# Attention with exact row maxima: 4 of a group's 32 maxima units are read as one difference and one sum

## What is computed

```python
q = split_heads(_tlin(x, w_q, s_q, b_q))        # (8, 16 heads, 1024, 16)
k = split_heads(_tlin(x, w_k, s_k, b_k))
v = split_heads(_tlin(x, w_v, s_v, b_v))
scores = jnp.einsum('bhqd,bhkd->bhqk', q, k) / jnp.sqrt(jnp.float32(HEAD))
attn = jax.nn.softmax(scores, axis=-1)
ctx = jnp.einsum('bhqk,bhkd->bhqd', attn, v)
```

## Time and profile before

| | before |
|---|---|
| median of three executions | 1980.98 us |
| span of the profiled execution | 1981.5 us |
| TensorE busy | 1931.0 us (97%) |
| VectorE busy | 1845.4 us (93%) |
| ScalarE busy | 1652.1 us (83%) |
| GpSimd busy | 750.0 us (38%) |
| granted TensorE clock, mean | 0.997 |

### The profile page before, as it was taken

How to read it: one execution, slowest core, us unless ns; L and a number is a source line. 1 busy time by engine, 2 the same in 40 slices (tenths; PEclk the granted TensorE clock), 3 DMA queues, 4 the chain that set the end, 5 groups by cost and what they waited for, 6 DMA issues and landing times.

```text
span 1981.5 us, 43034 instructions
## 1 busy us (share of the span) xinstructions
PE 1931.0 (97%) x15806; PEld 1131.4 (57%) x15806; DVE 1845.4 (93%) x3236; ACT 1652.1 (83%) x3241; POOL 750.0 (38%) x747
## 2 busy tenths in 40 slices
PE   8999999999999999999999999999999999999998
PEld 7766444444444444444444444444478888888876
DVE  4788999999999999999999999999289999999997
ACT  6655889899898989989898988988967777777776
POOL 3000364666575353010001001000046666666785
PEclk9999999999999999999999999999999999999999
DMA  7985553355435435433543544353011111111210
GB/s 224 284 236 209 120 76 52 62 95 96 94 81 102 95 80 99 93 94 82 101 96 78 97 94 94 82 100 98 28 49 49 49 49 49 49 49 56 63 33 27
DMA packets 127199, 181.46 MB, mean 92 GB/s; under 512 B 37836, under 2 KB 82636, under 8 KB 126988
## 3 DMA queue, kind: packets, MB, share of 16 engines
q1 hardware_dynamic: 119308, 171.10, 37.6%
q10 hardware_dynamic: 7392, 7.34, 1.1%
q0 software_dynamic: 288, 0.27, 0.1%
HBM read 103.68 MB, written 73.40 MB: 89 GB/s over the span
## 4 chain that ended last, share of the span: by engine, by line
DVE 63%; PE 32%; issue 3%; DMA 1%; ACT 1%; SPq 0%; DVEq 0%; POOLq 0%; POOL 0%; ACTq 0%
DVE halfmax L1135 50%; PE ps L1401 10%; DVE halfmax L1130 7%; PE ps L1440 6%; PE ps L494 4%; PE ps L504 3%; PE ps L1389 2%; PE ps L1412 2%; PE ps L1045 1%; PE ps L1011 1%; PE ps L481 1%; PE ps L1448 1%; DVE room L1591 1%; PE ps L1457 1%; DVE room L1678 1%
## 5 line engine op out<-in xcount | busy, mean ns | idle before, releaser
L1096 ACT ACTIVATE room<-ps 128x512 f32<-128x512 f32 x2048 | 1084.4, 600 | 125.0 <-PE ps L1011 103.0
L1135 DVE TENSOR_REDUCE halfmax<-ps 128x1 f32<-128x512 f32 x1714 | 1039.5, 676 | 1.3 <-PE ps L986 1.3
L1011 PE MATMUL ps<-qs,ks 50*128 50x512 f32 x2048 | 716.4, 448 | 2.4 <-DVE halfmax L1135 1.3
L986 PE MATMUL ps<-ks,qs 48*128 48x512 f32 x1960 | 667.6, 437 | 23.8 <-DVE halfmax L1130 22.3
L1045 PE MATMUL ps<-room,vals 128*17 128x256 f32 (+2 forms) x8192 | 578.9, 384 | 0.3 <-ACT craw L1104 0.3
L986 PEld LDWEIGHTS ps<-ks,qs 48*128 48x128 f32 x1960 | 314.5, 185 | 423.6 <-DVE halfmax L1135 309.2
L164 POOL CAST mrow<-turned_rows 128x32 fp32r<-128x32 f32 x32 | 6.7, 210 | 904.2 <-DVE turned_rows L159 695.4
L1011 PEld LDWEIGHTS ps<-qs,ks 50*128 50x128 f32 x2048 | 327.2, 184 | 22.9 <-ACT room L1096 14.5
L1045 PEld LDWEIGHTS ps<-room,vals 128*17 128x17 f32 x8192 | 167.4, 96 | 232.9 <-issue 168.1
L1401 PE MATMUL ps<-wguT,xqT 128*128 128x512 f32 (+1 forms) x1152 | 268.4, 386 | 3.9 <-DVE xqT L1631 3.9
L1401 PEld LDWEIGHTS ps<-wguT,xqT 128*128 128x128 f32 x1152 | 212.0, 189 | 51.8 <-issue 9.9
(11 more groups left out here) (116 smaller groups left out, 2212.1 us busy)
## 6 DMA issues: line engine op xcount, KB each, us to landing
qk_parts<-parts SPq DMA_DIRECT2D x64, 512.0 KB, 3.9
qs<-qk_parts SPq DMA_DIRECT2D x192, 128.0 KB, 4.4
ks<-qk_parts SPq DMA_DIRECT2D x192, 128.0 KB, 7.1
ctx_raw<-craw SPq DMA_DIRECT2D x64, 256.0 KB
ready<-passing SPq DMA_DIRECT2D x27, 512.0 KB, 6.5
pairs<-ready SPq DMA_DIRECT2D x27, 512.0 KB
out_dram<-fin SPq DMA_DIRECT2D x64, 128.0 KB, 1.7
xin<-in_L_attn_x_dram ACTq DMA_DIRECT2D x14, 512.0 KB, 5.4
```

What stands on the lines that cost most here:

```text
L986: nc.tensor.matmul(ps[:, MX + max_number(i, u, bank) % 4, :], qs[rows, i.slot(RING), pair, t * P:(t + 1) * P], ks[rows, i.slot(RING), pair ...
L1011: nc.tensor.matmul(ps[:, score_bank(i, s, n), :], ks[rows, slot, pair, kt * P:(kt + 1) * P], qs[rows, slot, pair, qh * BANK:(qh + 1) * BAN ...
L1096: nc.scalar.activation(prob[:, prob_slot(i, s), score_order(i, s)[n], :], ps[:, score_bank(i, s, n), :], ACT.Exp, scale=float(D) ** -0.5). ...
L1135: nc.vector.tensor_reduce(halfmax[:, i.slot(2), bank, column:column + 1], ps[:, at + bank, :], AX.X, ALU.max, negate=True).then_inc(max_re ...
```

## The change

Units 1, 9, 17 and 25 of groups 2 to 31 are handled in another way ("folded", `FOLD_PER = 8`, `FOLD_AT = 1`): 120 units in all, none of them among the units whose two banks are read in one reduce.

- TensorE makes bank 0 with two products into the same bank: the negated queries (`minus_q`) with the second half of the keys, then the queries with the first half. The bank holds the difference first minus second. Bank 1 is made as before.
- ScalarE takes the positive part of bank 0 (Relu) into `excess` in SBUF, between the third and the fourth exponential of the step. That also releases bank 0 to TensorE.
- VectorE waits for that and for bank 1, and with one instruction over 512 elements adds both, negates the sum and reduces it to its minimum, which is the negated maximum of all 1024 scores. The two reduces of the unit are gone. The other column of `halfmax` is set to a large number once.
- GpSimd negates the queries of the upper half of the rows once for each group (`minus_q`, 48 x 1024 elements), behind the wait for that group's stack and ahead of the wait for the turned maxima of the group before. Its first call of `next_maxima` now stands behind the wait for the projections.

```diff
+    minus_q = sb("minus_q", [P, 2, S], F32R)
+    excess = sb("excess", [P, 2, BANK])
...
+    def folded(i, u):
+        return i.k > 1 and u % FOLD_PER == FOLD_AT
...
+    def bank_read(eng, tile):
+        k, u = units_in_order[tile // QH]
+        if folded(At(None, k, RING), u) and tile % QH == 0:
+            eng.wait_ge(excess_ready, fold_number[k, u] + 1)
+        else:
+            eng.wait_ge(max_read, reads_done[tile])
...
             if max_number(i, u, bank) >= 4:
-                pe.wait_ge(max_read, reads_done[max_number(i, u, bank) - 4])
+                bank_read(pe, max_number(i, u, bank) - 4)
...
+            if folded(i, u) and bank == 0:
+                pe.wait_ge(minus_ready, i.k - 1)
+                nc.tensor.matmul(ps[:, MX + max_number(i, u, bank) % 4, :],
+                                 minus_q[rows, i.slot(2), t * P:(t + 1) * P],
+                                 ks[rows, i.slot(RING), pair, BANK:2 * BANK], start=True, stop=False)
+                nc.tensor.matmul(ps[:, MX + max_number(i, u, bank) % 4, :],
+                                 qs[rows, i.slot(RING), pair, t * P:(t + 1) * P],
+                                 ks[rows, i.slot(RING), pair, 0:BANK],
+                                 start=False, stop=True).then_inc(max_psum, 1)
+                return
...
+        def first_over_second(i, u):
+            n = fold_number[i.k, u]
+            act.wait_ge(max_psum, max_number(i, u, 0) + 1)
+            if n >= 2:
+                k, before = folds[n - 2]
+                act.wait_ge(max_read, reads_done[max_number(At(None, k, RING), before, QH - 1)])
+            nc.scalar.activation(excess[:, n % 2], ps[:, MX + max_number(i, u, 0) % 4, :],
+                                 ACT.Relu).then_inc(excess_ready, 1)
...
+                ahead, unit = maxima(i, s)
+                if i.k >= 0 and ahead.ok(NGR) and folded(ahead, unit + 1):
+                    exps(j, t, range(first, GH - 1))
+                    first_over_second(ahead, unit + 1)
+                    first = GH - 1
...
+        def take_folded(i, u):
+            column, at = max_column(u), MX + max_number(i, u, QH - 1) % 4
+            n = fold_number[i.k, u]
+            dve.wait_ge(excess_ready, n + 1)
+            dve.wait_ge(max_psum, max_number(i, u, QH - 1) + 1)
+            nc.vector.tensor_tensor_reduce(excess[:, n % 2], ps[:, at, :], excess[:, n % 2], -1.0, LARGE, ALU.add,
+                                           ALU.min, halfmax[:, i.slot(2), 0, column:column + 1]).then_inc(max_read, 1)
...
+            if i.k > 1:
+                dve.wait_ge(neutral, 1)
...
+                if i.k == 0 and s == ST - AHEAD + 2:
+                    columns = [max_column(u) for k, u in folds if k == folds[0][0]]
+                    nc.vector.memset(halfmax[:, :, 1, columns[0]:columns[-1] + 1:columns[1] - columns[0]],
+                                     LARGE).then_inc(neutral, 1)
...
+        def negate(i):
+            rows = slice(HALF, HALF + KR)
+            pool.wait_ge(stack_in[i.slot(RING)], i.turn(RING, LOADS, LOADS))
+            pool.wait_ge(maxima_out.parted, 2 * group[0])
+            wait(pool, passing_ready, 2 * max(0, min(group[0] - 1 - NG, READY)))
...
+            nc.gpsimd.tensor_scalar(minus_q[rows, i.slot(2), :], qs[rows, i.slot(RING), 0, :].bitcast(F32), -1.0, None,
+                                    ALU.mult).then_inc(minus_ready, 1)
+            pool.wait_ge(minus_ready, i.k - 1)
...
         def next_maxima():
+            if group[0] + 1 < NGR:
+                negate(At(None, group[0] + 1, RING))
             maxima_out.part(nc, pool, At(None, group[0], RING))
...
+        projections_done(pool)
         next_maxima()
-        projections_done(pool)
```

More of the change, by code:

```diff
@@ L54 @@
 FILL = 3
+FOLD_PER = 8
+FOLD_AT = 1
+LARGE = 3.0e38
 TILES_RUN = NTILES + 9
@@ L773, in attend @@
     wgu = sb("wgu", [WB, 2, 8, H])
+    minus_q = sb("minus_q", [P, 2, S], F32R)
+    excess = sb("excess", [P, 2, BANK])
+    minus_ready = sem("minus_ready")
+    excess_ready = sem("excess_ready")
+    neutral = sem("neutral")
     max_psum = sem("max_psum")
@@ L892, in max_number @@
         return QH * item[i.k, u] + bank
+    def folded(i, u):
+        return i.k > 1 and u % FOLD_PER == FOLD_AT
+    fold_number = {which: n for n, which in enumerate((k, u) for k, u in items() if folded(At(None, k, RING), u))}
+    folds = list(fold_number)
+    units_in_order = list(items())
     def read_table():
@@ L898, in read_table @@
         for k, u in items():
-            if whole(At(None, k, RING), u):
+            if whole(At(None, k, RING), u) or folded(At(None, k, RING), u):
                 table += [reads + 1, reads + 1]
@@ L1172, in vector @@
                         take_max(j, u, range(QH))
+                    elif j.ok(NGR) and folded(j, u):
+                        take_folded(j, u)
                     elif j.ok(NGR):
@@ L1176, in vector @@
                         whole_max(i.plus(1))
-                    if j.ok(NGR) and not whole(j, u):
+                    if j.ok(NGR) and not whole(j, u) and not folded(j, u):
                         take_max(j, u, [1])
@@ L1203, in pass_pair @@
             last.then_inc(passing_ready, 1)
+        def negate(i):
[3 more added lines that the diff above has]
+            wait(pool, passing_ready, 2 * max(0, min(group[0] - 1 - NG, READY)))
+            if i.k >= 4:
+                which = [n for n in folds if n[0] == i.k - 2][-1]
+                pool.wait_ge(max_psum, max_number(At(None, which[0], RING), which[1], 0) + 1)
+            nc.gpsimd.tensor_scalar(minus_q[rows, i.slot(2), :], qs[rows, i.slot(RING), 0, :].bitcast(F32), -1.0, None,
+                                    ALU.mult).then_inc(minus_ready, 1)
+            pool.wait_ge(minus_ready, i.k - 1)
         def next_maxima():
+            if group[0] + 1 < NGR:
+                negate(At(None, group[0] + 1, RING))
             maxima_out.part(nc, pool, At(None, group[0], RING))
```

## The result

The changed kernel takes 2035.82 us (median of four, 2034.07 to 2036.65) against 1981.67 us of the kernel before in the same comparison: ratio 1.0271, 95% interval 1.0259 to 1.0283. It is slower by 54 us. The forecast was 2030 us, in a range of 1985 to 2056.

What follows compares the result with a forecast made beforehand. TensorE's order with ScalarE's ring of three banks was taken to bind most of a group, VectorE only at double reads. Four stretches' delays, 1.66 us a group over 30 groups, added 49.8 us: 2030 us, range 1985 to 2056.

Steps and rivals of the forecast that it cites:

- The ceiling of 1.2 us a group: TensorE waits for VectorE some 1.2 us a group, at double reads; a faster VectorE alone gives 36 us.
- the walk: Step-by-step timing of one block, then of each fold's chain through TensorE, ScalarE and VectorE, from the profile's start times.
- The two stretches with ScalarE's ring: Units 9 to 17 and 25 to 1: Relu delays the last exponential TensorE's pair waits for, 0.41 us each.
- The two stretches with the double read: Units 17 to 25 and 1 to 9: late VectorE delays the pair after the double read, 0.6 and 0.24 us.
- The sum: The four stretches' delays added: 0.41 + 0.6 + 0.24 + 0.41 = 1.66 us a group, 49.8 us.
- the signs named beforehand: VectorE idle 0.6 to 1.1 us ahead of each sum, some 100 us in all; a period near 40.1 us.
- The sum instruction: VectorE's one instruction per fold replaces two reads: slot 0.70 us, bounds 0.60 and 0.95; work falls 2.0 us a group.
- The product: TensorE's extra product per fold shifts everything behind it by 0.24 us, bounds 0.21 and 0.34; 0.94 us a group.
- rival (a): VectorE's sum of work decides: 8 us gained, 1973, or 1922 if all TensorE's waits are VectorE's; 12 in 100.
- Rival (b): Unseen 0.1 to 0.3 us in ScalarE's ring absorbs the Relu's delay; gain and cost cancel, 1977 to 1985; 9 in 100.
- (d): VectorE's sum instruction takes a double slot, 1.2 us: 30 us more, 2060; 7 in 100.
- (e): Relu swaps ScalarE's tables, two loads of 1.28 us a fold: 308 us, 2340; 1 in 100.

Runs made afterwards that it cites:

- one_read: Kernel before, with VectorE's read of bank 0 left out in units 1, 9, 17 and 25, no extra product or Relu: 1947.5 us.
- relu_only: Kernel before, plus an unused Relu on ScalarE between the third and fourth exponential of the steps with units 1, 9, 17 and 25: 2000.6 us.
- no_relu: Changed kernel without the Relu; the sum takes a buffer of zeros instead and waits for bank 1 alone: 1967.8 us.
- spread_4: Changed kernel with a folded unit's bank 1 made and read four banks after bank 0; two double reads move to units 2 and 18: 2014.5 us.
- relu_first: Changed kernel with the Relu ahead of the step's third exponential and no longer behind it: 2003.4 us.
- spread_9: Changed kernel with folds at units 9 and 25 alone, bank 1 four banks behind bank 0, Relu ahead of the fourth exponential: 1997.0 us.
- spread_9_last: Changed kernel with folds at units 9 and 25 alone, bank 1 four banks behind bank 0, Relu behind the fourth exponential: 1997.6 us.

## Why the prediction was right

**The bound.** The ceiling of 1.2 us a group is what one_read measured, 1.11, and in the stretches where the walk had found the waits. Had the busy times and the chain been taken at their word, 2.0 us a group less work would have read as a gain of 60 us. But the prediction set VectorE's pace against TensorE's waits as if only one could hold: VectorE's work did set the length of the group, and it is the second bound 1.1 us below that limits the gain.

**The two stretches with ScalarE's ring** (0.41 us each in the sum) came out at 0.55 and 0.52. The walk had the next block's last pair at 2.38 us; the means over the groups are 2.43 and 2.38, where they were 1.97 and 1.97. Before the change the ring did not quite hold that pair, as the prediction read it: in the mean it started 0.16 us behind the end of the exponential, where pairs that do wait start 0.05 us behind. What the walk left out lies right behind that pair. It said that from there all is 0.41 us later, but from that pair to the first pair of the next block it is 1.20 us now and was 1.11. The pair's score product used to start 0.23 us behind the one before it and took 0.40 us; now it starts 0.49 us or more behind it and takes 0.50 (644.71 above), and the products with the values start 0.43 us after it and no longer 0.33 (means of both traces; relu_only has the same numbers as the changed kernel). The absolute 10.1 fell only 0.07 and 0.03 short of 10.17 and 10.13 because the one group walked had 9.70 before, above the mean of 9.62.

**The two stretches with the double read** (0.6 and 0.24) came out at 0.51 and 0.21; 10.0 was forecast for the one and 9.99 is measured for both. The pair released by the double read is at 5.06 in the mean, near the 5.10 forecast; before it was at 4.54 and not at the 4.46 of the group walked, so the step was 0.1 us smaller.

**The sum** was 1.66 us a group, 49.8 us; it is 1.79 and 54 us. The mechanism was right in all four stretches, and the signs named beforehand came: 0.93 us of idle time ahead of each sum, 111.6 us in all, and a group of 40.28 us for some 40.1. That the total came within 4 us is in part luck: 0.25 us too little in two stretches and 0.12 too much in the other two.

**The sum instruction** was costed at 0.70 us a slot, and its slot is 0.61: the read of the accumulator lies beside the next reduce. The 0.09 us too much count in the stretches with a double read; at unit 17 a sum that starts 0.03 us later than forecast (1.98 for 1.95) takes a third of them back. The Trainium skill (Vector Engine (DVE) Microarchitecture Reference, Points that are easy to get wrong) says that one form of instruction with two SBUF sources that are not bf16 has half the rate. No run here has a sum with two SBUF sources; with one source in PSUM it takes 692 ns against the reduce's 681. Relu brought no table load: the trace of the changed kernel has two, as the one before, at the start and at the Silu, and none in attention.

**The product** was the term furthest off. I took 0.94 us a group of TensorE off the ceiling and wrote that this left 0.3 us; rival (a) made 8 us of it. It measured 0.18 us a product, and alone it costs the group 0.08, since the stretches share VectorE's reserve. Without the Relu the change gains 14 us.

**Where the time is**, as a ladder of group lengths, each rung one thing more: before 38.49; all relief that VectorE can use, 37.38 (one_read); with product and sum instruction, 38.05 (no_relu); with the Relu on ScalarE but without VectorE's wait for it, 39.58 (spread_4, in which the double reads moved as well); with the wait, 40.28. So -1.11, +0.67, +1.53, +0.70. The rungs hold in this order; taken in another order the parts would differ, as the runs with one part alone show (0.61 for the Relu alone). GpSimd's negation is in no_relu too, and no wait for it shows.

Rival (a) falls with the result: VectorE has less to do and the kernel is slower. Rival (b), gain and cost cancel, falls with relu_first: the slot of 0.485 us by which the Relu is earlier comes back as 0.46 us in each of the two stretches. Rivals (d) and (e) fall with the 692 ns and the missing loads.

## What to carry to other kernels

An engine with no idle time and most of the chain can set the pace, and relieving it can still give little, as the next bound may lie close beneath: look at what releases each product of the other engine, stretch by stretch, and take only the waits for the busy engine as the ceiling of what relieving it can give. Work added elsewhere, up to that distance, is then hidden, as the product's was. When a step is handed to a third engine, walk the whole loop (make, convert, reduce, make again) against the time that the ring of buffers gives, and look for every engine that waits for an instruction behind the new one; sums of busy time have no place for either. A small instruction's cost can be mostly its position, as the Relu's 19 us against 2 for one place in the order shows; once another engine waits for its result the same move gains nothing (spread_9 and spread_9_last, 1997.0 and 1997.6 us).

## What the runs showed of the hardware that I had not expected

The accumulator read behind VectorE's sum (83 ns) starts in the same moment as the next reduce, 644.81 us, so it takes nothing from VectorE's pace. The extra product costs 0.18 us where it shows, less than the 0.23 us between the starts of two pairs in the same block (642.33 to 642.56). And a score product that no longer starts right behind another one is 0.50 us long in place of 0.40, which makes what follows in its block 0.1 us later.
